# State 0 of the selective scan split into two halves of the tokens, the first half issued in the scan's prologue

## The chip, the core and the metric

The kernel runs on one core of a Trainium2 chip. The time is the device time of one launch in microseconds; smaller is better. The core has five engines that each work through their own queue in order and meet at semaphores: TensorE (PE), VectorE (DVE), ScalarE (ACT), GpSimd (POOL) and SyncE (SP, which only issues DMAs here).

## What is computed

The reference is six residual blocks on x of 4 sequences x 256 tokens x 128 features: a linear attention, a cross attention, a two-pass mixture of experts, a selective state-space scan, a second cross attention and a quantised feed-forward. The change lies in the scan, whose reference is

```python
def _L1_attn_ref(x, W_xproj, W_dt, b_dt, A_log, D):
    proj = x @ W_xproj
    dt_inter = proj[..., :DT_RANK]
    B_ssm = proj[..., DT_RANK:DT_RANK + STATE]
    C_ssm = proj[..., DT_RANK + STATE:]
    delta = jax.nn.softplus(dt_inter @ W_dt + b_dt)
    A = -jnp.exp(A_log)
    log_delta_A = jnp.clip(delta[..., None] * A[None, None], LOG_EPS, CLAMP)
    delta_A = jnp.exp(log_delta_A)
    delta_B_u = delta[..., None] * B_ssm[:, :, None, :] * x[..., None]
    log_dA = jnp.log(jnp.clip(delta_A, 1e-07, None))
    log_R = jnp.cumsum(log_dA, axis=1)
    R = jnp.exp(jnp.minimum(log_R, CLAMP))
    exp_neg_log_R = jnp.exp(jnp.minimum(-log_R, CLAMP))
    S = jnp.cumsum(delta_B_u * exp_neg_log_R, axis=1)
    h = R * S
    y = jnp.einsum('bln,bldn->bld', C_ssm, h) + x * D
    return y
```

STATE is 16: for each of 16 states and each of 128 features a recurrence runs along the 256 tokens of each sequence.

## The kernel before

The 128 features lie on the partitions and the 1024 tokens (4 sequences of 256) along the free dimension. A "half" is 512 tokens, two whole sequences, which is also one bank of PSUM; DELTA, DX, XNT, DA, DXB, CARRY, FLOOR and ROW are all 128 x 1024, and no recurrence crosses from one half to the other. Names of tiles in the profile are those of the memory they lie in: DELTA, DX and LA are parts of SCR, DA and FIRST_STEP of OT, BC, BCOL and DXB of KSA, HH, CCOL and the scratch of the rows of VA, HC of E, and ROW, FLOOR, CARRY and Y are pairs of banks of PS.

**Prologue**, once for each half. It begins when that half's tokens have been normalised by DVE (line 1780), turned by PE (1787) and copied to XNT by ACT (1792). PE projects them to the 64 step inputs (1958), ACT copies these (1979), PE makes four copies of the 32 rows of B and C (1966) and projects the steps to delta (1974). ACT computes the exp and ln of the softplus (1985, 1987, 1988). DVE splits the rows into three bfloat16 parts in BC (2006, 2007, 2011, 2017, 2018, 2019), adds up delta (2025, 2032) and multiplies it by the input into DX (2038). The first half's prologue is done while the experts' last steps still run, apart from lines 2032 and 2038; the second half's stands in front of the scan.

**The loop** goes over the states n = 0 to 15. For each n ACT makes the decays DA = exp(delta * A[n]) (2117) and writes the four entries of FLOOR that start the sequences (2111, out of FIRST_STEP, which lines 2185, 2121 and 2189 prepare for all states at once); POOL clamps DA (2144); DVE carries the reciprocal of the product along with a scan (2201), multiplies it by the input product DXB (2207) and runs the second scan, the state itself (2214). PE spreads one row of B or C over all partitions (356, called by `row`), ACT copies it out of PSUM (2098, 2105), POOL forms the next state's DXB (2151) and the output product (2159), which PE adds up over the states (2061). Only for state 0 does DVE itself form DXB, straight from PSUM (2195).

The order on each engine is the order in which the code is written (`scan_tensor`, `scan_scalar`, `scan_pool`, `scan_vector` and the engines' main lists at the end of the file). On PE, `turn_over` (line 345) issues matmuls whose result nobody reads; 20 of them stand between the end of the experts and the turning of the last half. In DVE's list for state 0 the order is

```python
carry(0); first_input(); accumulate(0); advance(0)
```

and PE's first row of state 1 waits for `dxb`, that is for `first_input`, since it overwrites the banks that this reads.

## Time and profile before

| | us |
|---|---|
| median of 3 runs | 564.98 |
| lowest and highest of them | 563.54, 565.07 |
| profiled execution, its time | 563.37 |
| its span, first to last instruction | 561.6 |
| DVE busy in the span | 448.7 |
| PE busy in the span | 481.0 |
| ACT busy in the span | 277.6 |
| POOL busy in the span | 202.9 |

The profiled execution is the lower end of the runs, 1.61 us under their median; 1.77 us of its time lie around the span. The experts end at about 307.5 us of the span, the scan's loop lies between 325.4 and about 422 us. A busy share says little about such a stretch: several engines hand work to each other there, and the question at each point is which of them was waited for last. All times in the rows further down are microseconds from the span's start.

### The profile page before, as it was taken

The numbers are of one execution on the slowest core, as the hardware profiler recorded it, in microseconds if no ns is written. First come the engines' busy times: TensorE is split into PE (matmuls) and PEld (weight loads), VectorE is DVE, ScalarE is ACT, GpSimd is POOL, SyncE is SP. The second block draws the span as 40 slices with busy tenths as digits, with TensorE's granted clock in tenths as the row PEclk, the third lists the DMA queues.
The fourth block names the chain that finished last, engine by engine and source line by source line (L and its number), as shares of the span: only waits on it lengthen the run. The fifth ranks groups of instructions, "written<-read, shape, count | busy, mean of one in ns | idle before, by whom it ended". The sixth has DMA issues, their size and how long they took to land.

```text
span 561.6 us, 9242 instructions
## 1 busy us (share of the span) xinstructions
PE 481.0 (86%) x3108; PEld 281.3 (50%) x3117; DVE 448.7 (80%) x1176; ACT 277.6 (49%) x517; POOL 202.9 (36%) x170
## 2 busy tenths in 40 slices
PE   7889899999998999899989636656679999999866
PEld 6444666666555666566555102212224656666423
DVE  7998867776587567375886799999996889998996
ACT  3740356555543234345243246555421477777655
POOL 8724000000002305332500048999990255543130
PEclk9999899999999999999999856788789999999989
DMA  5510260000010302422100000000001000000001
GB/s 147 146 39 1 73 191 2 2 1 2 1 48 9 98 11 70 115 61 61 55 0 2 1 0 0 0 0 1 1 0 47 2 2 2 1 3 2 1 1 39
DMA packets 25392, 17.34 MB, mean 31 GB/s; under 512 B 2977, under 2 KB 24162, under 8 KB 25346
## 3 DMA queue, kind: packets, MB, share of 16 engines
q1 hardware_dynamic: 24322, 14.65, 9.2%
q0 software_dynamic: 1024, 2.10, 1.2%
q8 instruction: 26, 0.43, 0.3%
q14 instruction: 20, 0.16, 0.1%
HBM read 10.06 MB, written 5.51 MB: 28 GB/s over the span
## 4 chain that ended last, share of the span: by engine, by line
PE 32%; DVE 16%; POOL 12%; issue 6%; ACT 3%; DMA 1%; SPq 0%; DVEq 0%; POOLq 0%; ACTq 0%
PE PS L1343 7%; PE PS L814 5%; POOL E L2159 4%; PE PS L1385 4%; PE PS L859 3%; POOL KSA L2151 3%; PE PS L876 3%; DVE PS L2201 2%; PE PS L2061 1%; POOL OT L2617 1%; POOL OT L2144 1%; DVE VA L2214 1%; POOL sorted L2607 1%; PE PS L345 1%; PE PS L834 1%
## 5 line engine op out<-in xcount | busy, mean ns | idle before, releaser
L859 PE MATMUL PS<-QM,KP 32*128 32x256 f32 x512 | 91.8, 398 | 1.2 <-ACT E L1047 0.8
L814 PE MATMUL PS<-KP,QP 32*128 32x256 f32 x512 | 78.0, 400 | 0.2 <-ACT QP L1025 0.2
L1047 ACT ACTIVATE E<-PS 128x512 f32<-128x512 f32 x100 | 56.1, 595 | 34.9 <-PE PS L859 24.3
L2607 POOL DMA_INDIRECT sorted<-VA,slot_of x16 | 15.7, 981 | 146.6 <-DVE expert_at L1737 129.6
L859 PEld LDWEIGHTS PS<-QM,KP 32*128 32x128 f32 x512 | 60.5, 184 | 6.2 <-issue 4.8
L356 PE MATMUL PS<-KSA,select 128*128 128x512 bf16 x62 | 25.2, 495 | 40.9 <-ACT KSA L2098 29.1
L1343 PE MATMUL PS<-XNT,KSA 128*128 128x512 f32 x128 | 58.6, 596 | 0.0
L814 PEld LDWEIGHTS PS<-KP,QP 32*128 32x128 f32 x512 | 51.3, 184 | 14.4 <-issue 10.0
L1122 DVE CUSTOM_DVE_ANT_0 SCR<-PS,KSA 128x256 f32<-128x256 f32 x128 | 47.5, 419 | 9.1 <-PE PS L814 8.3
L1117 DVE TENSOR_REDUCE MXT<-PS 128x2 f32<-128x512 f32 x64 | 41.0, 685 | 15.5 <-PE PS L814 15.5
L2582 POOL TENSOR_TENSOR VA<-VA,KSA 128x512 f32<-128x512 f32 x28 | 35.2, 1277 | 37.7 <-ACT VA L1052 37.7
L1351 ACT ACTIVATE E<-PS 128x512 f32<-128x512 f32 x32 | 18.8, 596 | 46.7 <-PE PS L1343 46.7
L2061 PE MATMUL PS<-E,ident 128*128 128x512 f32 x60 | 36.8, 748 | 2.0 <-POOL E L2159 2.0
L2201 DVE TENSOR_TENSOR_SCAN PS<-OT,PS 128x1024 f32<-128x1024 f32 x16 | 36.7, 2295 | 1.4 <-ACT PS L2111 0.8
L356 PEld LDWEIGHTS PS<-KSA,select 128*128 128x128 bf16 x64 | 5.1, 108 | 64.7 <-ACT KSA L2098 39.0
L2151 POOL TENSOR_TENSOR KSA<-SCR,KSA 128x1024 f32<-128x1024 f32 x15 | 35.2, 2348 | 4.8 <-ACT KSA L2098 4.8
L2159 POOL TENSOR_TENSOR E<-VA 128x1024 f32<-128x1024 f32 x15 | 35.3, 2350 | 2.5 <-PE PS L2061 1.5
L1357 DVE TENSOR_TENSOR E<-E,PS 128x512 f32<-128x512 f32 x32 | 21.9, 685 | 17.4 <-ACT E L1351 15.8
L1385 PEld LDWEIGHTS PS<-KSA,E 128*128 128x128 f32 x256 | 30.7, 192 | 10.1 <-issue 9.8
L2144 POOL TENSOR_SCALAR OT<-OT 128x1020 f32<-128x1020 f32 x16 | 16.7, 1042 | 50.7 <-ACT OT L2117 49.6
L2214 DVE TENSOR_TENSOR_SCAN VA<-OT,PS 128x1024 f32<-128x1024 f32 x15 | 34.3, 2286 | 0.5
L345 PE MATMUL PS<-wq,identb 128*128 128x512 bf16 x130 | 34.3, 398 | 0.4 <-issue 0.2
(334 smaller groups left out, 1049.4 us busy)
## 6 DMA issues: line engine op xcount, KB each, us to landing
KSA<-in_w SPq DMA_DIRECT2D x2, 1024.0 KB, 7.0
sorted<-zeros SPq DMA_DIRECT2D x2, 960.0 KB, 6.4
answers<-OT SPq DMA_DIRECT2D x14, 128.0 KB, 1.8
KSA<-in_w SPq DMA_DIRECT2D x2, 512.0 KB, 9.7
QP<-sorted SPq DMA_DIRECT2D x4, 256.0 KB, 3.0
QP<-sorted SPq DMA_DIRECT2D x2, 448.0 KB, 4.7
X<-in_x SPq DMA_DIRECT2D x2, 256.0 KB, 3.3
SCR<-in_ctxT SPq DMA_DIRECT2D x1, 512.0 KB, 6.0
```

Source lines behind the costliest of these rows:

```text
L345: pe.matmul(bank(bk), identb[:, :], wq1[:, :], start=True, stop=True)
L814: ins = pe.matmul(score_bank(n, i)[:, q * S:(q + 1) * S], QP[rows(i), g, t:t + P], KP[rows(i), g, b * S:(b + 1) * S], start=True, stop=Tru ...
L859: ins = pe.matmul(o[:, kt * S:(kt + 1) * S], KP[rows(i), g, t:t + P], QM[rows(i), g, b * S:(b + 1) * S], start=True, stop=True, skip_group ...
L1047: act.activation(slot(m, j), drain_bank(L, m, j), ACT.Exp).then_inc(sig("exps"), 1)
L1117: ins = dve.tensor_reduce(MXT[:, n % 2, :, c], o, AX, ALU.max, negate=True)
L1122: ins = dve.tensor_tensor_reduce(out=BIASED[:, i % 2, q, :], in0=o[:, q, :], in1=BIASQ[:, q, :], scale=-1.0, scalar=3e38, op0=ALU.add, op1 ...
L1343: ins = pe.matmul(unit_bank(g, o), w[:, e, c * P:(c + 1) * P], XNT[:, tokens_of(p)], start=True, stop=True)
L1385: ins = pe.matmul(bank(6)[:, t * P:(t + 1) * P], E6[:, (2 * m + c) % 4, t * P:(t + 1) * P], W2[:, m % NE, c, :], start=(c == 0), stop=(c = ...
L2061: ins = pe.matmul(bank(6 + half), ident[:, :], HC[n % 2][:, half * HALF:(half + 1) * HALF], start=(n == 0), stop=False, skip_group_check=True)
L2151: pool.tensor_tensor(DXB[n % 2], DX, BCOL[n % 2], ALU.mult).then_inc(sig("dxb"), 1)
L2159: pool.tensor_tensor(HC[n % 2], HH[n % 2], CCOL[n % 2], ALU.mult).then_inc(sig("outputs"), 1)
L2201: dve.tensor_tensor_scan(CARRY, DA[n % 3], FLOOR, 0.0, ALU.mult, ALU.add).then_inc(sig("carried"), 1)
```

## The change

State 0's chain is written out by halves. `first_log`, `first_max`, `first_input` and `first_carry` on DVE, `first_step`, `first_decay` and `first_half` on ACT, `first_clamp` on POOL and `scan_first_row` on PE each do one half, 512 tokens or two sequences, of what one instruction did for all 1024. The first half of each is issued in the prologue: on PE right after the experts, on ACT before the second half's softplus, on DVE before the second half's rows are split. The second half stands where the whole stood, but that DVE's carried scan comes behind `scan_rows_tail` together with `first_input`. Three banks of the second half's prologue move to make room (`SCAN_BANK`), and the counts that the later waits ask for go up by one. States 1 to 15 are as before.

```diff
-        SCAN_BANK = ((7, 7, 7), (0, 4, 1))
+        SCAN_BANK = ((7, 7, 7), (1, 6, 7))
...
+        def scan_first_row(pe, half):
+            pe.wait_ge(sig("bc_rows"), half + 1)
+            pe.matmul(bank(half), select[:, 0:1].to_broadcast([P, P]), BC[:, tokens_of(half)], start=True, stop=True)\
+                .then_inc(sig("row_psum"), 1)
+
...
-            pe.wait_ge(sig("bc_rows"), 2)
-
             def row(k, r):
 
                 if k == 1:
-                    pe.wait_ge(sig("dxb"), 1)
-                elif k:
+                    pe.wait_ge(sig("dxb"), 2)
+                else:
                     pe.wait_ge(sig("row_read"), k - 1)
                 project(pe, 0, select[:, r:r + 1].to_broadcast([P, P]), BC, "row_psum")
...
-            row(0, 0)
+            scan_first_row(pe, 1)
             row(1, 1)
...
-            scan_steps_take(act, 1)
-            scan_softplus(act, ch, 1)
...
-                act.wait_ge(sig("row_psum"), n + 1 + max(n - 1, 0))
+                act.wait_ge(sig("row_psum"), n + 2 + max(n - 1, 0))
                 if n >= 2:
-                    act.wait_ge(sig("dxb"), n - 1)
+                    act.wait_ge(sig("dxb"), n)
...
+            def first_step(half):
+                act.wait_ge(sig("first_log"), half + 1)
+                s = FIRST_STEP[:, :, 2 * half:2 * half + 2]
+                act.activation(s, s, ACT.Exp, bias=ssmc[:, 2:3]).then_inc(sig("first_exp"), 1)
+
+            def first_decay(half):
+                act.wait_ge(sig("delta"), half + 1)
+                b = slice(2 * half, 2 * half + 2)
+                act.activation(inner(DA[0])[:, b, :], inner(DELTA)[:, b, :], ACT.Exp, scale=amat[:, 0:1])\
+                    .then_inc(sig("decay"), 1)
+
+            def first_half(half):
+                act.wait_ge(sig("first_max"), half + 1)
+                b = slice(2 * half, 2 * half + 2)
+                act.activation(starts(FLOOR)[:, b, :], FIRST_STEP[:, 0, b].unsqueeze(2), ACT.Copy)\
+                    .then_inc(sig("first"), 1)
+
             def first(n):
 
-                if n:
-                    act.wait_ge(sig("carried"), n)
+                act.wait_ge(sig("carried"), n + 1)
...
-            act.wait_ge(sig("first_log"), 1)
-            act.activation(FIRST_STEP, FIRST_STEP, ACT.Exp, bias=ssmc[:, 2:3]).then_inc(sig("first_exp"), 1)
-            act.wait_ge(sig("delta"), 2)
-            decay(0)
-            act.wait_ge(sig("first_max"), 1)
-            first(0)
+            first_step(0)
+            first_decay(0)
+            first_half(0)
+            scan_steps_take(act, 1)
+            scan_softplus(act, ch, 1)
+            first_step(1)
+            first_decay(1)
+            first_half(1)
             decay(1)
             b_copy(1)
             c_copy(0)
...
+            def first_clamp(half):
+                pool.wait_ge(sig("decay"), half + 1)
+                a = inner(DA[0])[:, 2 * half:2 * half + 2, :]
+                pool.tensor_scalar(a, a, GUARD, LOWEST, ALU.min, ALU.max).then_inc(sig("da"), 1)
+
             def clamp(n):
 
-                pool.wait_ge(sig("decay"), n + 1)
+                pool.wait_ge(sig("decay"), n + 2)
...
-            clamp(0)
+            first_clamp(0)
+            first_clamp(1)
             pool.wait_ge(sig("dx"), 2)
...
+            def first_log(half):
+                b = slice(2 * half, 2 * half + 2)
+                dve.tensor_tensor(FIRST_STEP[:, :, b],
+                                  starts(DELTA)[:, b, :].rearrange("p b o -> p o b").to_broadcast([P, NS, 2]),
+                                  amat[:, :].unsqueeze(2).to_broadcast([P, NS, 2]), ALU.mult).then_inc(sig("first_log"), 1)
+
+            def first_max(half):
+                s = FIRST_STEP[:, :, 2 * half:2 * half + 2]
+                dve.wait_ge(sig("first_exp"), half + 1)
+                dve.tensor_scalar(s, s, LOWEST * GUARD, None, ALU.max).then_inc(sig("first_max"), 1)
+
+            def first_input(half):
+                t = tokens_of(half)
+                dve.wait_ge(sig("row_psum"), half + 1)
+                dve.wait_ge(sig("dx"), half + 1)
+                dve.tensor_tensor(DXB[0][:, t], DX[:, t], bank(half), ALU.mult).then_inc(sig("dxb"), 1)
+
+            def first_carry(half):
+                t = tokens_of(half)
+                dve.wait_ge(sig("da"), half + 1)
+                dve.wait_ge(sig("first"), half + 1)
+                dve.tensor_tensor_scan(CARRY[:, t], DA[0][:, t], FLOOR[:, t], 0.0, ALU.mult, ALU.add)\
+                    .then_inc(sig("carried"), 1)
+
+            scan_delta(dve, 0)
+            first_log(0)
             ch.link(dve.memset(FLOOR, 0.0))
-            scan_delta(dve, 0)
             scan_drive(dve, 0)
+            first_max(0)
+            first_input(0)
+            first_carry(0)
             scan_rows_head(dve, ch, 1)
             scan_positive(dve, ch, 1)
             scan_rows_middle(dve, 1)
             scan_delta(dve, 1)
-            dve.tensor_tensor(FIRST_STEP, starts(DELTA).rearrange("p b o -> p o b").to_broadcast([P, NS, B]),
-                              amat[:, :].unsqueeze(2).to_broadcast([P, NS, B]), ALU.mult).then_inc(sig("first_log"), 1)
+            first_log(1)
             scan_drive(dve, 1)
-            dve.wait_ge(sig("first_exp"), 1)
-            dve.tensor_scalar(FIRST_STEP, FIRST_STEP, LOWEST * GUARD, None, ALU.max).then_inc(sig("first_max"), 1)
+            first_max(1)
             scan_rows_tail(dve, ch, 1)
-
-            def first_input():
-                dve.wait_ge(sig("row_psum"), 1)
-                dve.wait_ge(sig("dx"), 2)
-                dve.tensor_tensor(DXB[0], DX, ROW, ALU.mult).then_inc(sig("dxb"), 1)
+            first_carry(1)
+            first_input(1)
 
...
-                dve.wait_ge(sig("da"), n + 1)
-                dve.wait_ge(sig("first"), n + 1)
+                dve.wait_ge(sig("da"), n + 2)
...
-                dve.wait_ge(sig("carried"), n + 1)
-                dve.wait_ge(sig("dxb"), n + 1)
+                dve.wait_ge(sig("carried"), n + 2)
+                dve.wait_ge(sig("dxb"), n + 2)
...
-                carry(n)
-                if n == 0:
-                    first_input()
+                    carry(n)
                 accumulate(n)
...
@@ -2773,6 +2819,7 @@
             self_tensor(pe)
             cross_tensor(pe, 0)
             experts_tensor(pe)
+            scan_first_row(pe, 0)
             turn_over(pe, 1, 20)
             half_turn(pe, 1, 5)
             turn_over(pe, 1, 2)
```

The queue of DVE between the normalisation of the last half (1780) and the split of its rows (2006, 2007). Names left of the arrow are the output's memory; a scan is printed as SCALAR_TENSOR_TENSOR.

```order
 L1780 TENSOR_SCALAR XN<-X,mv,rstd 128x128 x4
-L2178 MEMSET PS 128x1024
 L2032 TENSOR_TENSOR SCR<-SCR 128x512
+L2205 TENSOR_TENSOR OT<-SCR,amat 128x16x2
+L2229 MEMSET PS 128x1024
 L2038 TENSOR_TENSOR SCR<-SCR,XNT 128x512
+L2212 TENSOR_SCALAR OT<-OT 128x16x2
+L2218 TENSOR_TENSOR KSA<-SCR,PS 128x512
+L2224 SCALAR_TENSOR_TENSOR PS<-OT,PS 128x512
 L2006 CAST KSA<-PS 128x512
 L2007 TENSOR_TENSOR VA<-PS,KSA 128x512
```

Four instructions (the first half of FIRST_STEP's product and maximum, of the input product, and of the carried scan) have come in ahead of line 2006. The memset of FLOOR is the same one, one place later.

The queue of DVE from the second half's middle rows to state 0's accumulation, before and then changed:

```order
L2011 CAST VA<-VA 128x512
L2032 TENSOR_TENSOR SCR<-SCR 128x512
L2185 TENSOR_TENSOR OT<-SCR,amat 128x64
L2038 TENSOR_TENSOR SCR<-SCR,XNT 128x512
L2189 TENSOR_SCALAR OT<-OT 128x64
L2017 COPY KSA<-VA 32x512
L2018 TENSOR_TENSOR VA<-VA 128x512
L2019 COPY KSA<-VA 32x512
L2201 SCALAR_TENSOR_TENSOR PS<-OT,PS 128x1024
L2195 TENSOR_TENSOR KSA<-SCR,PS 128x1024
L2207 SCALAR_TENSOR_TENSOR PS<-PS,KSA 128x1024
```

```order
L2011 CAST VA<-VA 128x512
L2032 TENSOR_TENSOR SCR<-SCR 128x512
L2205 TENSOR_TENSOR OT<-SCR,amat 128x16x2
L2038 TENSOR_TENSOR SCR<-SCR,XNT 128x512
L2212 TENSOR_SCALAR OT<-OT 128x16x2
L2017 COPY KSA<-VA 32x512
L2018 TENSOR_TENSOR VA<-VA 128x512
L2019 COPY KSA<-VA 32x512
L2224 SCALAR_TENSOR_TENSOR PS<-OT,PS 128x512
L2218 TENSOR_TENSOR KSA<-SCR,PS 128x512
L2255 SCALAR_TENSOR_TENSOR PS<-PS,KSA 128x1024
```

The number of instructions is the same; four of them are half as wide.

The queue of ACT from the copy of the last half into XNT to the end of the prologue:

```order
 L1792 ACTIVATE XNT<-PS 128x512
+L2111 ACTIVATE OT<-OT,ssmc 128x16x2
+L2116 ACTIVATE OT<-SCR,amat 128x2x255
+L2122 ACTIVATE PS<-OT 128x2
 L1979 ACTIVATE SCR<-PS 64x512
 L1985 ACTIVATE SCR<-PS,ssmc 128x512
 L1987 ACTIVATE SCR<-SCR 128x512
 L1988 ACTIVATE SCR<-SCR 128x512
-L2121 ACTIVATE OT<-OT,ssmc 128x64
-L2117 ACTIVATE OT<-SCR,amat 128x4x255
-L2111 ACTIVATE PS<-OT 128x4
```

Three instructions have come in ahead of line 1979, and behind 1988 the same three stand again for the other half. On POOL two clamps of 128 x 510 stand in the place of one of 128 x 1020.

## Rows read from the trace of the kernel before

**Rows 1.** The page's first line.

```profile
span 561.6 us, 9242 instructions
```

**Rows 2.** Busy time by stage: stretch, length, busy by engine, granted clock, DMA share, GB/s.

```profile
313.70:318.50 4.80, 4.77 (x17) 1.44 (x18) 2.30 (x3) 1.19 (x2) 0.00 (x0) 0.64 0.00 0
333.40:420.00 86.60, 54.10 (x116) 18.78 (x119) 85.06 (x45) 45.68 (x57) 82.09 (x44) 0.78 0.00 0
```

**Rows 3.** The chain of waits, 313 to 334 us: start, length, piece.

```profile
315.57 1.89 PE PS L1958 x2
...
324.37 0.88 issue
...
328.97 1.05 PE PS L356 x2
...
330.04 1.03 ACT KSA L2098
```

**Rows 4.** Waits of DVE, 325 to 420 us: in total, times, longest.

```profile
DVE PS L2201 <- ACT PS L2111: 0.8, 1, 0.8
```

**Rows 5.** The timeline of DVE, 313 to 330 us.

```profile
313.88 0.91 DVE L2178 MEMSET PS<- 128x1024 f32 x1 [0.21 <-issue]
...
318.52 0.69 DVE L2006 CAST KSA<-PS 128x512 bf16<-128x512 f32 x1 [2.21 <-PE PS L1966]
...
320.27 0.75 DVE L2025 TENSOR_SCALAR SCR<-PS,ssmc 128x512 f32<-128x512 f32 x1 [0.33 <-ACT SCR L1985]
...
322.31 0.26 DVE L2185 TENSOR_TENSOR OT<-SCR,amat 128x64 f32<-128x64 f32 x1
...
323.60 0.69 DVE L2018 TENSOR_TENSOR VA<-VA 128x512 bf16<-128x512 f32 x1
324.33 1.00 DVE L2019 COPY KSA<-VA 32x512 bf16<-32x512 bf16 x1
325.37 2.30 DVE L2201 TENSOR_TENSOR_SCAN PS<-OT,PS 128x1024 f32<-128x1024 f32 x1
327.69 1.22 DVE L2195 TENSOR_TENSOR KSA<-SCR,PS 128x1024 f32<-128x1024 f32 x1
329.02 1.23 DVE L2207 SCALAR_TENSOR_TENSOR PS<-PS,KSA 128x1024 f32<-128x1024 f32 x1
```

**Rows 6.** The timeline of ACT and of POOL, 313 to 325 us.

```profile
314.76 0.60 ACT L1792 ACTIVATE XNT<-PS 128x512 f32<-128x512 f32 x1 [3.10 <-PE PS L1787]
317.56 0.59 ACT L1979 ACTIVATE SCR<-PS 64x512 f32<-64x512 f32 x1 [2.20 <-PE PS L1958]
...
322.86 1.13 ACT L2117 ACTIVATE OT<-SCR,amat 128x1020 f32<-128x1020 f32 x1
...
324.07 2.24 POOL L2144 TENSOR_SCALAR OT<-OT 128x1020 f32<-128x1020 f32 x2 [48.62 <-ACT OT L2117]
```

**Rows 7.** Single lines: duration in ns min/median/max, first and last start, forms.

```profile
L2230 DVE TENSOR_TENSOR_SCAN VA<-OT,PS x2: 1194/1207/1220, 419.9 to 421.0; 128x512 f32<-128x512 f32 x2
...
L2019 DVE COPY KSA<-VA x2: 285/645/1005, 306.7 to 324.3; 32x512 bf16<-32x512 bf16 x2
...
L2144 POOL TENSOR_SCALAR OT<-OT x16: 1037/1037/1122, 324.1 to 411.9; 128x1020 f32<-128x1020 f32 x16
```

**Rows 8.** The timeline at 251 us: POOL and DVE side by side, then DVE's next.

```profile
251.30 0.61 POOL L2758 TENSOR_SCALAR KSA<-SCR 128x512 f32<-128x512 f32 x1
251.33 0.59 DVE L269 TENSOR_TENSOR rt<-rs 128x4 f32<-128x4 f32 x1 [0.18 <-POOL rs L2625]
...
251.95 0.16 DVE L270 TENSOR_TENSOR rt<-rt,ve 128x4 f32<-128x4 f32 x1
```

**Rows 9.** The timeline of PE behind the loop, and the clock there by stretches.

```profile
423.04 1.88 PE L2080 MATMUL PS<-E,ident 128*128 128x512 f32 x4
...
416.30:419.70 3.40, 3.18 (x6) 1.09 (x6) 3.37 (x2) 0.20 (x1) 3.40 (x2) 0.50 0.00 0
419.70:426.00 6.30, 6.10 (x22) 2.77 (x21) 4.98 (x7) 0.00 (x0) 1.57 (x2) 1.00 0.00 0
```

More of the change, by code:

```diff
@@ L2089, in scan_scalar @@
         def scan_scalar(act, ch):
-            scan_steps_take(act, 1)
-            scan_softplus(act, ch, 1)
             def b_copy(n):
-                act.wait_ge(sig("row_psum"), n + 1 + max(n - 1, 0))
+                act.wait_ge(sig("row_psum"), n + 2 + max(n - 1, 0))
                 if n >= 2:
-                    act.wait_ge(sig("dxb"), n - 1)
+                    act.wait_ge(sig("dxb"), n)
                 act.activation(BCOL[n % 2], ROW, ACT.Copy).then_inc(sig("row_read"), 1)
             def c_copy(n):
-                act.wait_ge(sig("row_psum"), b_rows(n + 1) + n + 1)
+                act.wait_ge(sig("row_psum"), b_rows(n + 1) + n + 2)
                 if n >= 2:
@@ L2184, in scan_vector @@
             scan_delta(dve, 1)
-            dve.tensor_tensor(FIRST_STEP, starts(DELTA).rearrange("p b o -> p o b").to_broadcast([P, NS, B]),
-                              amat[:, :].unsqueeze(2).to_broadcast([P, NS, B]), ALU.mult).then_inc(sig("first_log"), 1)
+            first_log(1)
             scan_drive(dve, 1)
-            dve.wait_ge(sig("first_exp"), 1)
-            dve.tensor_scalar(FIRST_STEP, FIRST_STEP, LOWEST * GUARD, None, ALU.max).then_inc(sig("first_max"), 1)
+            first_max(1)
             scan_rows_tail(dve, ch, 1)
-            def first_input():
-                dve.wait_ge(sig("row_psum"), 1)
-                dve.wait_ge(sig("dx"), 2)
-                dve.tensor_tensor(DXB[0], DX, ROW, ALU.mult).then_inc(sig("dxb"), 1)
+            first_carry(1)
+            first_input(1)
             def carry(n):
-                dve.wait_ge(sig("da"), n + 1)
-                dve.wait_ge(sig("first"), n + 1)
+                dve.wait_ge(sig("da"), n + 2)
+                dve.wait_ge(sig("first"), n + 2)
                 dve.tensor_tensor_scan(CARRY, DA[n % 3], FLOOR, 0.0, ALU.mult, ALU.add).then_inc(sig("carried"), 1)
             def accumulate(n):
-                dve.wait_ge(sig("carried"), n + 1)
-                dve.wait_ge(sig("dxb"), n + 1)
+                dve.wait_ge(sig("carried"), n + 2)
+                dve.wait_ge(sig("dxb"), n + 2)
                 dve.scalar_tensor_tensor(CARRY, CARRY, 1.0, DXB[n % 2], ALU.min, ALU.mult).then_inc(sig("input"), 1)
```

## The prediction

> **What bounds the kernel now.** I read the page's span first (561.6 us, [rows 1]), then the stages around the change, then the chain of waits through them, then each engine's timeline where the chain changes hands. In the scan's loop, 333.4 to 420 us, DVE is busy for 85.06 of 86.60 us and POOL for 82.09, PE for 54.10 [rows 2]: DVE sets the pace and POOL is close behind. DVE waits once in it, 0.8 us for ACT's line 2111 ahead of state 1's first scan [rows 4]. So the loop is a rigid block: whoever starts it earlier ends it earlier, and what follows hangs on its end.
>
> In front of the loop DVE is not the pace-maker all the time. Behind line 2038 of the first half it sits idle for 2.21 us until PE's four copies of the rows arrive at 318.52 [rows 5]. In that gap PE runs L1958 for 1.89 us [rows 3], at a granted clock that averages 0.64 over 313.70 to 318.50 [rows 2]. Before line 2025 DVE idles another 0.33 us, for ACT [rows 5]. From 322 us on DVE is on the chain without a pause: the copy of line 2019 (1.00 us), state 0's first scan (2.30), the input product of line 2195 (1.22), and 2207 starts at 329.02 [rows 5]. The end of 2195 also releases PE's first row of state 1 (328.97, 1.05 us), ACT's copy (330.04, 1.03 us), one more row and copy, and so state 1 [rows 3]. What ends 2195 earlier therefore moves the whole rest.
>
> **The copy of line 2019.** It has a price of its own kind. The same 32 x 512 copy took 285 ns in the first half and 1005 ns in the second [rows 7]; the second time POOL's clamp ran from 324.07 [rows 6], for 1.122 us, the longest of 16 [rows 7], so to 325.19, and the copy ended at 325.33, 0.14 behind it. The chain calls 0.88 us of it "issue" [rows 3]: DVE stood still with its instruction issued. The other order is in the rows too: line 2018 (0.69 us, from 323.60) had begun before the clamp, and it was the clamp that took 1.122 instead of 1.037 us [rows 5, 7]. Whoever begins first goes on; the second stands.
>
> **The change, part by part.**
>
> *First half on DVE, ahead of line 2006.* Added work: half of line 2185 (0.26 for 64 columns, so 0.2), half of 2189 (0.2), an input product of 128 x 512 (0.69, as line 2018, the nearest two-operand row of that width [rows 5]), and a scan of 128 x 512, 1.19 us by line 2230 [rows 7]. Sum 2.3 us, plus some 0.03 us between instructions: about 2.4. The cover is the 2.21 us gap and the 0.33 us behind it [rows 5]. Step by step, with DVE starting where it did (313.88): delta to 314.6, product 314.8, memset (0.91) to 315.75, drive to 316.5. Meanwhile ACT is free at 315.36, behind line 1792 [rows 6]; its exp of the starts takes 0.3 and the half decay 0.6 (a 128 x 512 ACT row is 0.60, a 128 x 1020 one 1.13 [rows 6]), so DA's first half stands at 316.3 and POOL clamps it to 316.95 at 0.61 us, the price of a 128 x 512 tensor_scalar [rows 8]. DVE: maximum 316.55 to 316.7, input product to 317.4, scan to 318.65; line 2006 then begins at 318.65 instead of 318.52. These 0.13 us go into the 0.33 us of idle in front of line 2025 [rows 5]. ACT's three added pieces end at 316.9, before PE has the steps for line 1979 at 317.56 [rows 6]. **Net zero on the path.** The cover has a hole: if POOL's clamp begins before DVE's maximum, the maximum stands until some 316.85 and line 2006 slips to 319.0; 0.2 of the 0.5 us would show. PE's added matmul stands in front of 20 that nobody reads and a wait, so at nothing. It might even help there: if that bit of work kept the clock from averaging 0.64 over the stretch [rows 2], L1958 would take half a microsecond or more less and line 2006 could come up to 0.3 us earlier, as soon as DVE is through with its added work. Bounds: nothing, or 0.3 us gained; I take nothing, since the work is small.
>
> *The copy of line 2019.* ACT's decay of the second half now starts at 322.8 and ends 0.5 us sooner (0.6 in the place of 1.13 us [rows 6]), at 323.4; POOL begins its half clamp at 323.5, 0.07 before line 2018 would begin (323.57: the narrower product of line 2185 saves 0.03). I take it that line 2018 gets through first, since POOL's clamp was slowed by 0.085 us while 0.22 us of it lay beside line 2018 [rows 5, 7], so that it seems to need the memory only 0.1 us or so after its start. Then 2018 ends at 324.26, the clamp at 324.7, and the copy at 324.83 to 324.88: **0.45 us earlier** than 325.33. Were there no clash at all it would end at 324.6 (0.73 earlier); the other bound is the first rival.
>
> *Half a scan.* In place of 2.30 us [rows 5] a scan of 1.19 [rows 7]: **1.1 us less**.
>
> *Half an input product.* In place of 1.22 a product of 0.69 [rows 5]: **0.53 us less**. PE's row for it needs BC at 324.9 and one matmul of about 0.5 us (two took 1.05 [rows 3]), ready at 325.5, while DVE's half scan lasts until 326.1.
>
> Sum: 0.45 + 1.1 + 0.53 = 2.1 us, so line 2207 begins at 326.9. The chain of rows and copies to state 1 hangs on the input product and moves by the same 2.1; so do DVE's 0.8 us of waiting there and everything of POOL's. POOL's first full clamp then lies at 324.7 to 325.8, beside a scan; line 2201 took its 2.30 us beside the second clamp, and half a scan was 1.19 [rows 5, 7], so it was not slowed. No queue is refilled and no DMA is moved: SP's list is the same. **What is late next** is the same handover to state 1.
>
> Against its own time the profiled execution would come to 563.37 - 2.1 = 561.3 us. It lies 1.6 under the median of the three runs; against that median the forecast is 564.98 - 2.1 = **562.9 us**, 0.37% less.
>
> **A rule to weigh.** The trace shows a DVE instruction with two operands in SBUF, the tiny line 269, taking 0.59 us beside a POOL tensor_scalar that had begun 0.03 us earlier, where its neighbour of the same shape took 0.16 [rows 8]. The Trainium skill, "SBUF — State Buffer", section "Who interferes with whom", says that a VectorE instruction with both inputs in SBUF contends with a GpSimd instruction that reads SBUF, and that the one that begins second is fully blocked. Line 2018 is such an instruction. By the row of the old kernel, where it came first, the sum is 2.1; by the rule with POOL's half clamp first, it is that of the first rival.
>
> **The rivals.**
>
> *1. Line 2018 and the copy both lose to POOL.* The half clamp now becomes ready 0.07 us before line 2018, where the whole one came 0.47 us after its start (324.07 against 323.60 [rows 5, 6]). If POOL wins, line 2018 stands until about 324.0 and ends at 324.7; by then ACT has the decay of state 1 ready (1.13 us from 323.5), POOL's full clamp can begin at 324.73, and if it beats the copy by a hair, that ends 0.14 us behind it, at 325.9. The scan starts 1.0 us later than forecast, the gain is 1.1: 563.9 us. For it: three starts within 0.1 us. Against: it takes two lost races in a row; with the first alone the gain is 2.0.
>
> *2. The first half is not covered.* If the half clamp costs the full clamp's 1.04 us [rows 7] and the maximum stands behind it, DVE's scan ends at 319.4, line 2006 starts 0.9 us late and some 0.7 shows: gain 1.4, 563.6 us. Against: the 0.61 us of [rows 8] for half the columns.
>
> *3. The loop does not follow.* State 1 would be held by something that has not moved, and the change gives nothing: 565.0 us. I find no such thing; everything that state 1 waits for comes behind the input product [rows 3].
>
> *4. Slower: the clock behind the loop.* PE's matmuls that end the sums stand on the path: L2080's four took 1.88 us, and L2061's four before them the same, at a granted clock of 1.00, which rose from 0.50 at 419.7 [rows 9]. The changed kernel brings them 2.1 us nearer to where the clock was low. If it rises only behind them, they cost twice: 3.8 us more, against 2.1 gained, so 1.7 slower, 566.7 us; it decides from 2.1 us on, when more than half of them run at 0.50. For it: only 1.6 us lie between the rise and the first of them. Against: the matmuls that nobody reads in front of them are what kept PE busy for 3.18 of the 3.40 us before the clock rose [rows 9], and they move along.
>
> **How the numbers follow.** Forecast 0.62 (561.0 to 563.6 with the runs' own spread of 1.5 us), rival 1 0.15, rival 2 0.12, rival 3 0.05, rival 4 0.06. The range must reach over rivals 1 and 2, and below to the profiled execution's 561.3 and the 0.3 us that PE's clock might add: 561.0 to 564.7. About 0.3%, 1.7 us, is what a measurement of this kernel tells from no change. The forecast lies only 0.4 us beyond it. Faster: nearly all of the forecast (0.58) and a little of rival 2: 0.60. Same: the rest of the forecast, rivals 1 to 3: 0.34. Slower: rival 4, 0.06.
>
> **What would show it.** In the changed trace: line 2006 within 0.2 us of 4.64 us behind the first DVE instruction after the normalisation (318.52 against 313.88 [rows 5]) and no DVE idle of 2.2 us before it; the scan of line 2224's second half starting about 324.9 and the accumulation at 326.9, on this time axis; the second copy of line 2019 at 0.5 us or so instead of 1.00; the loop's length unchanged. Wrong would be: the copy at 1 us again or line 2018 above 0.69 (rival 1); line 2006 late by more than 0.3 (rival 2); a wait of DVE inside the loop that was not there (rival 3); the eight fp32 matmuls behind the loop above 1.88 us a group (rival 4).

## The result and the profile after

The changed kernel takes 560.11 us (median of 10 runs, 558.89 to 561.56), the kernel before, on the same chip, 563.92 (10 runs, 561.85 to 565.07): ratio 0.993, 95% interval 0.9913 to 0.9946. That is faster, by 3.8 us where 2.1 were forecast. Both kernels were run again three times: the medians were 563.6 to 563.9 us for the old one and 559.8 to 560.1 for the new one. A few executions of the runs below took 632 us or more; they are in no median and no ratio.

One view of each engine carries the comparison. First the timeline of DVE in the changed kernel; it answers to [rows 5] (columns as there):

```profile
311.46 1.12 DVE L1780 TENSOR_SCALAR XN<-X,mv,rstd 128x128 f32<-128x128 f32 x4
...
313.62 0.91 DVE L2229 MEMSET PS<- 128x1024 f32 x1 [0.21 <-issue]
...
315.17 0.59 DVE L2212 TENSOR_SCALAR OT<-OT 128x32 f32<-128x32 f32 x1
315.67 0.68 DVE L2218 TENSOR_TENSOR KSA<-SCR,PS 128x512 f32<-128x512 f32 x1
316.27 1.22 DVE L2224 TENSOR_TENSOR_SCAN PS<-OT,PS 128x512 f32<-128x512 f32 x1
317.40 0.67 DVE L2006 CAST KSA<-PS 128x512 bf16<-128x512 f32 x1
...
318.71 0.74 DVE L2025 TENSOR_SCALAR SCR<-PS,ssmc 128x512 f32<-128x512 f32 x1
...
319.83 0.69 DVE L2032 TENSOR_TENSOR SCR<-SCR 128x512 f32<-128x512 f32 x1
...
321.77 0.69 DVE L2018 TENSOR_TENSOR VA<-VA 128x512 bf16<-128x512 f32 x1
322.49 0.58 DVE L2019 COPY KSA<-VA 32x512 bf16<-32x512 bf16 x1
323.10 1.23 DVE L2224 TENSOR_TENSOR_SCAN PS<-OT,PS 128x512 f32<-128x512 f32 x1
324.36 0.69 DVE L2218 TENSOR_TENSOR KSA<-SCR,PS 128x512 f32<-128x512 f32 x1
325.16 1.23 DVE L2255 SCALAR_TENSOR_TENSOR PS<-PS,KSA 128x1024 f32<-128x1024 f32 x1
...
329.55 2.30 DVE L2249 TENSOR_TENSOR_SCAN PS<-OT,PS 128x1024 f32<-128x1024 f32 x1 [0.83 <-ACT PS L2128]
```

The 2.21 us of idle in front of line 2006 are gone, and so is the 0.33 in front of 2025: DVE works from the normalisation to state 0's end almost without a pause (0.21 us at the memset). Line 2006 still stands 4.82 us behind the end of line 1780 (312.58), as before (318.52 - 313.68 = 4.84). The copy of line 2019 takes 0.58 us instead of 1.00. State 1's first scan begins 16.97 us behind the end of line 1780; in the old trace it was 19.74 (333.42 less 313.68). I call this **the stretch**; its 2.8 us are the change's own part. POOL's two half clamps and the first whole one, which answer to [rows 6]:

```profile
314.82 0.91 POOL L2162 TENSOR_SCALAR OT<-OT 128x510 f32<-128x510 f32 x1 [40.46 <-ACT OT L2116]
321.79 1.14 POOL L2162 TENSOR_SCALAR OT<-OT 128x510 f32<-128x510 f32 x1 [6.07 <-ACT OT L2116]
323.01 1.04 POOL L2168 TENSOR_SCALAR OT<-OT 128x1020 f32<-128x1020 f32 x1
```

Both half clamps began beside a DVE instruction with two operands in SBUF and took 0.3 and 0.5 us longer than the 0.61 that such a clamp took alone (its row stands with the run that has the zeros on ScalarE, below). DVE's maximum (line 2212, 0.59 us instead of 0.18) stood behind the first of them.

The timeline of PE ahead of and in the second half's prologue shows what the forecast had not counted:

```profile
306.44 4.48 PE L345 MATMUL PS<-wq,identb 128*128 128x512 bf16 x20
312.63 0.66 PE L1787 MATMUL PS<-ident,XN 128*128 128x128 f32 x4 [1.72 <-DVE XN L1780]
313.12 0.60 PE L345 MATMUL PS<-wq,identb 128*128 128x512 bf16 x2
314.07 1.04 PE L1958 MATMUL PS<-XNT,wssm 128*64 128x512 f32 x2 [0.35 <-ACT XNT L1792]
```

L1958's pair takes 1.04 us where it had taken 1.89 in the chain [rows 3]. The granted clock, by stretches as in [rows 2], is 1.00 here and was 0.64 there. By a **fall** of the clock I mean in what follows a time in which it is at 0.50, the lower of its two levels (1.2 of 2.4 GHz). The loop in the second row is unchanged (DVE 84.93 of 86.50 us):

```profile
312.58:317.40 4.82, 3.99 (x18) 1.23 (x18) 4.54 (x7) 2.10 (x5) 0.91 (x1) 1.00 0.01 2
...
329.50:416.00 86.50, 52.27 (x115) 18.51 (x119) 84.93 (x45) 45.59 (x57) 81.74 (x44) 0.80 0.00 0
```

DVE's waits from 311 to 416 us are the same one at state 1 as in [rows 4], and the memset's:

```profile
DVE PS L2249 <- ACT PS L2128: 0.8, 1, 0.8
DVE PS L2229 <- issue: 0.2, 1, 0.2
```

The matmuls behind the loop run as in [rows 9]: L2083, which was L2080, takes 1.88 us again.

```profile
419.41 1.88 PE L2083 MATMUL PS<-E,ident 128*128 128x512 f32 x4
```

The spans differ by 3.4 us (558.2 and 561.6). The stretch gives 2.8. Another 1.1 us were gained ahead of line 1780, where the code is the same, and 0.4 lost behind the loop.

### The profile page after: what moved, and what is told of

Read it like the earlier page. It is cut to its first block, busy times and chain, and to the rows that moved or that the text cites. A ratio compares the mean times of both kernels' runs of the same rounds, so it can differ in the third digit from the quotient of the medians.

```text
span 558.2 us, 9251 instructions
## 1 busy us (share of the span) xinstructions
PE 475.9 (85%) x3108; PEld 279.4 (50%) x3117; DVE 448.2 (80%) x1180; ACT 277.9 (50%) x520; POOL 203.8 (37%) x171
## 4 chain that ended last, share of the span: by engine, by line
PE 31%; DVE 21%; POOL 8%; issue 6%; ACT 3%; DMA 1%; SPq 0%; DVEq 0%; POOLq 0%; ACTq 0%
PE PS L1343 7%; PE PS L814 5%; PE PS L1385 4%; DVE PS L2249 3%; PE PS L859 3%; DVE VA L2262 3%; POOL E L2183 3%; PE PS L876 3%; POOL KSA L2175 2%; PE PS L2064 2%; DVE PS L2255 2%; POOL OT L2663 1%; POOL sorted L2653 1%; PE PS L834 1%; DMA answers<-OT 1%
## 5 line engine op out<-in xcount | busy, mean ns | idle before, releaser
L859 PE MATMUL PS<-QM,KP 32*128 32x256 f32 x512 | 91.9, 398 | 1.2 <-ACT E L1047 0.8
L859 PEld LDWEIGHTS PS<-QM,KP 32*128 32x128 f32 x512 | 60.6, 184 | 6.2 <-issue 4.8
L1122 DVE CUSTOM_DVE_ANT_0 SCR<-PS,KSA 128x256 f32<-128x256 f32 x128 | 47.5, 420 | 9.1 <-PE PS L814 8.3
L356 PE MATMUL PS<-KSA,select 128*128 128x512 bf16 x60 | 23.6, 481 | 35.4 <-ACT KSA L2099 30.7
L1351 ACT ACTIVATE E<-PS 128x512 f32<-128x512 f32 x32 | 18.8, 596 | 46.7 <-PE PS L1343 46.7
L2249 DVE TENSOR_TENSOR_SCAN PS<-OT,PS 128x1024 f32<-128x1024 f32 x15 | 34.4, 2295 | 1.3 <-ACT PS L2128 0.8
L876 PE MATMUL PS<-E,VX 128*32 128x256 f32 x512 | 34.3, 385 | 0.1
L1343 PEld LDWEIGHTS PS<-XNT,KSA 128*128 128x128 f32 x128 | 22.8, 191 | 22.7 <-issue 22.4
```

The lines of the kernel that those rows point to most:

```text
L859: ins = pe.matmul(o[:, kt * S:(kt + 1) * S], KP[rows(i), g, t:t + P], QM[rows(i), g, b * S:(b + 1) * S], start=True, stop=True, skip_group ...
L876: ins = pe.matmul(bank(6)[rows(i), (g % 2) * S:(g % 2) * S + S], VX[:, QT * b + kt, HG * g + i, :], slot(m, j)[:, kt * S:(kt + 1) * S], st ...
L1122: ins = dve.tensor_tensor_reduce(out=BIASED[:, i % 2, q, :], in0=o[:, q, :], in1=BIASQ[:, q, :], scale=-1.0, scalar=3e38, op0=ALU.add, op1 ...
L1343: ins = pe.matmul(unit_bank(g, o), w[:, e, c * P:(c + 1) * P], XNT[:, tokens_of(p)], start=True, stop=True)
L2249: dve.tensor_tensor_scan(CARRY, DA[n % 3], FLOOR, 0.0, ALU.mult, ALU.add).then_inc(sig("carried"), 1)
```

## The experiments

Three accounts were open: **moved work** (the forecast's 2.1 us, the rest chance), **the clock ahead of the last half** (worth something more because it stayed up), and something in **code that is the same**. A table of all runs comes at the end of this section.

### Both kernels again

> The kernel before, unchanged, timed against itself for the size of the noise. Three accounts of the 3.8 us are open. Moved work: 2.1 us come from half a scan, half a product and the shorter copy, and anything else is chance. Clock ahead of the last half: TensorE's clock fell to 0.50 at 313.9 us in the old trace and did not in the new one, worth 0.7 us where it falls. Early stretch: 1.5 us were gained at 41 to 47 us, where the code is the same. Chance would have this run's trace differ from the old one in those two places about as often as not, and the ratio 1.000 within 0.002. If the old kernel always falls there, this trace shows 0.50 at 40.8 to 44.2 and at 313.9 to 317.3 again.

> The changed kernel, unchanged. Moved work alone: about 2.1 us under the kernel before (0.996), in any trace from the end of line 1780 to state 1's first scan about 17.5 us where the clock has fallen and 17.0 where not. With a clock effect that is systematic: 3 to 4.5 us (0.992 to 0.995), 17.0 us in that stretch, and no fall of the clock at about 313.

No edit. The old kernel against itself: 1.0006 (0.9988 to 1.0025), the changed one 0.9921 (0.9891 to 0.9951). In the stretch the old kernel's clock had fallen again (19.8 us), the new one's had not (17.0); the fall at about 41 us, ahead of anything that the change touches, is in the first and fourth trace of the old kernel and in the second and third of the changed one, and in none of their other four. So what the early part of the kernel takes is chance: the end of line 1780 lay between 311.2 and 314.8 us in the four traces of the changed kernel, between 311.7 and 313.7 in the four of the old one. The fall at 41 us is one of three in that part, the others lie at about 11 and 57 us. In the one trace of the eight without any of them line 1780 ended at 311.2 us, in the four with one at 311.7 to 312.6, in the two with two at 313.7 and in the one with all three at 314.8.

### Filling TensorE's idle ahead of the last half

```diff
-            turn_over(pe, 1, 20)
+            turn_over(pe, 1, 28)
```

> The kernel before with 28 instead of 20 matmuls that nobody reads ahead of the turning of the last half, 8 x 0.21 us into TensorE's 1.9 us of idle. Clock ahead of the last half: the clock stays at 1.00, L1958's pair takes 1.0 instead of 1.9 us, the rows arrive 1.2 us earlier, and the kernel gains 0.7 to 1.2 us (about 0.998). Moved work only: 0, ratio 1.000; slower by up to 0.3 us if the last of them are in the way.

0.9969 (0.9945 to 0.9994) and a stretch of 18.5 us: no fall, line 2006 at 3.6 instead of 4.8 us behind the end of line 1780. The clock account holds: in the old kernel the fall costs 1.3 us of the stretch. (As a time the ratio says 1.7 us, with an interval from 0.3 to 3.1.) The same in the changed kernel, 27 for 20:

> The changed kernel with 27 instead of 20 such matmuls. If in the changed kernel the clock never falls there, the same time as the changed kernel within 0.3 us. If it falls in some executions, up to 0.5 us less. If the matmuls stand in the way of the turning, up to 0.3 us more.

0.9925 (0.9898 to 0.9952), stretch 17.0: nothing left to gain, as the clock was up already.

### How little it takes

> The kernel before with 21 instead of 20 matmuls that nobody reads ahead of the last half's turning: one matmul of 0.21 us more on TensorE, which is what the change puts there too with its row of state 0. If the change's extra gain comes from that one matmul: no fall of the clock ahead of the last half, the stretch from the end of line 1780 to state 1's first scan takes 18.5 us instead of 19.8, and the kernel gains 1.3 us (0.998), as with 28. If the change keeps the clock up by something else, the clock falls as before: 19.8 us and 1.000.

1.0001 (0.9981 to 1.0021), and the trace had the fall (stretch 20.1 us). By this the one matmul was nothing. It was tried again, and with 23:

> The kernel before with 21 instead of 20 matmuls that nobody reads, once more. Up to the turning of the last half TensorE then does exactly what it does in the changed kernel, whose clock stayed up there in 4 of 4 traces, as the old one's fell in 4 of 4. If the length of the idle (1.72 instead of 1.93 us) decides, this trace has no fall, 18.5 us for the stretch, and the ratio lies below 1 by some tenths of a per cent. If it falls again and the ratio is 1.000 again, the one matmul is not what keeps the clock up in the changed kernel.

> The kernel before with 23 such matmuls, 0.64 us more than before and 0.43 more than with 21. Between 21 (ratio 1.000) and 28 (0.997). If the idle's length decides, it is at 0.997 already and its trace has no fall (18.5 us); otherwise it lies between.

The second trace with 21 had no fall (18.5 us) and its ratio was 0.998 (0.9955 to 1.0005). With 23 it was **0.9941** (0.9919 to 0.9964), no fall. By that ratio three matmuls that nobody reads bring the old kernel 3.3 us, more than was expected and nearly what the change brings. But these are six executions with an interval from 2.0 to 4.6 us; the stretch of 18.5 us, the same as with 28, shows 1.3 of it, and the kernel with 28 gained 1.7. PE in the kernel with 23:

```profile
306.13 5.13 PE L345 MATMUL PS<-wq,identb 128*128 128x512 bf16 x23
312.54 0.66 PE L1787 MATMUL PS<-ident,XN 128*128 128x128 f32 x4 [1.28 <-DVE XN L1780]
...
313.97 1.04 PE L1958 MATMUL PS<-XNT,wssm 128*64 128x512 f32 x2 [0.35 <-ACT XNT L1792]
```

The idle of PE ahead of L1787 was 1.93 us in the old kernel, 1.72 with 21 and in the changed kernel, 1.28 with 23. Over all twenty traces: with 1.93 us the clock fell there in 4 of 6 (the four unchanged old kernels; not in the two with delays below, which are the same up to there), with 1.72 in 1 of 10, with less in 0 of 3; the kernel with 12 matmuls, below, had 3.44 us and the fall. By these counts one matmul more seems to make the fall rarer; it does not abolish it. The two traces without the fall at 1.93 us were taken on one chip and the old kernel's three repeated ones on two others, so chance and chip are not told apart here.

### The changed kernel with the clock down

```diff
-            turn_over(pe, 1, 20)
+            turn_over(pe, 1, 12)
```

> The changed kernel with 12 instead of 20 such matmuls: TensorE idles 1.7 us more ahead of the last half, so that the clock should fall there. If the moved work is worth 2.1 us at the old clock, as forecast, the stretch takes 17.7 us (19.8 less 2.1) against 17.0 now, and the kernel loses 0.7 us against the changed one: about 0.994 to 0.996 of the kernel before. If the stretch stays at 17.0, the clock has no part in it. If it takes 18.2 or more, the clock explains half of the whole gain.

0.9952 (0.9932 to 0.9972); stretch 17.57 us. This is the clean test of the forecast, since the clock is down here too (from about 312 us, with L1787 at 1.12 us and L1958's pair at 1.75). DVE's timeline:

```profile
311.31 1.12 DVE L1780 TENSOR_SCALAR XN<-X,mv,rstd 128x128 f32<-128x128 f32 x4
...
317.20 0.69 DVE L2006 CAST KSA<-PS 128x512 bf16<-128x512 f32 x1 [0.16 <-PE PS L1966]
...
318.94 0.75 DVE L2025 TENSOR_SCALAR SCR<-PS,ssmc 128x512 f32<-128x512 f32 x1 [0.33 <-ACT SCR L1985]
...
320.27 0.69 DVE L2032 TENSOR_TENSOR SCR<-SCR 128x512 f32<-128x512 f32 x1
```

The added work fits under the gap with 0.16 us to spare, the 0.33 us in front of line 2025 are back, and the stretch is 19.74 - 17.57 = **2.17 us** shorter than the old one, for a forecast of 2.1.

### The first half not moved

```diff
             first_max(0)
-            first_input(0)
-            first_carry(0)
             scan_rows_head(dve, ch, 1)
...
             scan_rows_tail(dve, ch, 1)
+            first_carry(0)
+            first_input(0)
             first_carry(1)
             first_input(1)
```

> The changed kernel with state 0's input product and carried scan of the first half put back behind the second half's rows: the same halves on the same engines, but nothing of DVE's big work moved into the prologue. Moved work: the line 2006 comes at once behind PE, 3.6 us behind the end of line 1780 instead of 4.8, state 0's accumulation comes later by 1.9 us less the 0.6 us that the second half's delta now comes sooner, so 1.3 us more in the stretch (18.3 us) and 1.3 us slower than the changed kernel. If the moved work were worth nothing and the clock all, the same time as the changed kernel.

0.996 (0.9939 to 0.9981), median 561.3 us; stretch 18.6. The halves alone bring the stretch nothing beside an old kernel with its clock up (18.5); moving them brings 1.6 us of it.

### FLOOR's zeros from ScalarE

```diff
-            ch.link(dve.memset(FLOOR, 0.0))
             scan_drive(dve, 0)
...
             norm_root(act, ch, 3, tiles_of(1))
+            ch.link(act.activation(PS[:, 2:4, :].rearrange("p a (b n) -> p (a b) n", b=4),
+                                   zeros[:, :].unsqueeze(1).to_broadcast([P, 8, P]), ACT.Copy))
```

> The changed kernel with FLOOR filled with zeros by ScalarE in its idle time ahead of the last half, instead of VectorE's memset of 0.91 us between the first half's product and drive. If the first half's added work does not fit under the gap once the clock stays up (line 1780 to the second half's delta is 7.25 us, and 6.66 in the filled kernel before), this gives back up to 0.6 us: the maximum no longer stands behind POOL's clamp (0.18 instead of 0.59 us), line 2006 comes at 4.1 instead of 4.8 us, delta at 6.7, the stretch takes 16.4 us. If the added work was covered, no change.

Each step came as expected: line 2006 at 4.1 us, delta at 6.7, the maximum no longer behind POOL, the stretch 16.45 us, 0.5 less. In its timeline the maximum and what follows it read

```profile
316.86 0.18 DVE L2212 TENSOR_SCALAR OT<-OT 128x32 f32<-128x32 f32 x1 [0.23 <-ACT OT L2111]
316.96 0.68 DVE L2218 TENSOR_TENSOR KSA<-SCR,PS 128x512 f32<-128x512 f32 x1
318.16 1.23 DVE L2224 TENSOR_TENSOR_SCAN PS<-OT,PS 128x512 f32<-128x512 f32 x1 [0.53 <-POOL OT L2162]
```

and the first half clamp, which here began beside no DVE instruction with two operands in SBUF,

```profile
317.52 0.61 POOL L2162 TENSOR_SCALAR OT<-OT 128x510 f32<-128x510 f32 x1 [40.53 <-ACT OT L2116]
```

The time did not follow: 0.9932 (0.9902 to 0.9961), the changed kernel's own. Half a microsecond is too small for these runs; in this trace 0.7 us were lost right behind the loop (see under the count). No version beat the changed kernel.

### Delays, for what lies behind the loop

The old kernel's three later traces had a second fall, in the end of the last cross attention, where the code is the same. PE's timeline in the fourth trace of the old kernel:

```profile
514.87 1.93 PE L876 MATMUL PS<-E,VX 128*32 128x256 f32 x16
516.73 1.11 PE L886 MATMUL PS<-ident,OT 128*128 128x128 f32 x4
```

And the clock there, by the view of stretches with the columns of [rows 2]:

```profile
514.20:517.60 3.40, 3.40 (x27) 1.55 (x24) 1.57 (x3) 2.69 (x5) 0.00 (x0) 0.57 0.01 2
```

In the changed kernel's first trace the same two lines take 1.07 and 0.66 us:

```profile
512.92 1.07 PE L876 MATMUL PS<-E,VX 128*32 128x256 f32 x16
513.93 0.66 PE L886 MATMUL PS<-ident,OT 128*128 128x128 f32 x4
```

PE was busy without a gap before this fall (9.20 of the 9.20 us from 505.00 to 514.20). What follows L834's last pair then takes 47.9 us instead of 46.4: 1.5 us. To see whether the moment at which a kernel gets there matters, both kernels were delayed in the loop:

```diff
+                if n in (2,):
+                    for j in range(NT):
+                        dve.bn_stats(st[:, j, :], X[:, j, :])
                 accumulate(n)
```

and once more with `(2, 5)`. Each delay turned out as 1.40 us of loop (from state 1's first scan to the end of the last one 88.76, 90.16, 91.55 us).

> The kernel before with 8 needless bn_stats on VectorE in the loop's state 2, a pure delay of 1.6 us on the engine that sets the pace. The traces so far show a second fall of TensorE's clock, at 512 to 517 us, in the end of the last cross attention, worth 1.3 us: in 2 of 3 traces of kernels that reach the loop like the old one, in none of the 3 like the changed one. Account with this fall (whether it comes depends on when the kernel gets there): a delay of 1.6 us moves the old kernel away from it, so the kernel loses only 0.5 to 1.0 us, and its trace has no fall there. Account without: it loses 1.6 us.

> The same delay twice (states 2 and 5), 3.2 us. With the fall: its effect comes and goes with the delay, so that here the old kernel meets it about as often as undelayed, and loses 3.2 us, that is 2.2 to 2.7 us more than with one delay. Without: 3.2 us as well, 1.6 more than with one.

> The changed kernel with the delay of 1.6 us. With the fall: this puts the changed kernel where the old one was, so the fall at about 515 us appears in its trace and it loses 1.6 plus up to 1.3, 2.3 to 2.9 us against the changed kernel (0.9975 to 0.999 of the kernel before). Without: it loses 1.6 us (0.996).

> The changed kernel with 3.2 us of delay. With the fall: it is gone again, the kernel loses 3.2 us against the changed one, only 0.3 to 0.9 more than with one delay. Without: 3.2 us, 1.6 more than with one.

The old kernel with 1.4 us of useless work was not slower: 0.9988 (0.997 to 1.0006). With 2.8 us it was at 1.0034 (1.001 to 1.0058), 1.9 us slower with an interval from 0.6 to 3.3. The changed kernel went from 0.993 to 0.9961 (0.9938 to 0.9984) and 0.9982 (0.9962 to 1.0002): 1.7 and 2.9 us for 1.4 and 2.8. So the account's half on the old kernel agrees with the times, and its half on the changed one does not agree with the traces: one delay did not bring the fall to the one that was taken (46.6 us behind L834), two did (48.0 us), against the expectation. One trace says little, though: of the eleven executions with one delay seven took 559.0 to 561.7 us and four 563.4 to 564.9, and the trace is of the first group. Neither delayed old kernel's trace had a fall, here or ahead of the last half. The place ahead of the last half was not in the delay's power, since it lies before it, so part of what the delays seem to have cost the old kernel too little is chance there.

### The count

> The kernel before once more, for its trace: which of the two falls of the clock it has. The falls account says that the old kernel meets one at 312 to 315 us or one at 512 to 517 us in most executions: the stretch from the end of line 1780 to state 1's first scan takes 19.8 (fall) or 18.5 us (none), and what follows L834's last turning of the maxima takes 47.9 (fall) or 46.5 us.

> As the run before it. If neither fall shows in these two traces and the medians stay at 563.8, the falls don't explain the 3.7 us, and 1.5 us of it are without a cause.

> The changed kernel once more, for its trace: 17.0 us for the stretch and 46.5 us for the end, both without a fall, 3.7 us under the kernel before. A fall at about 515 us here would say that the changed kernel meets it too, and its part of the gain would shrink.

> The changed kernel a fourth time, with the same two numbers expected: 17.0 us for the stretch and 46.5 us for the end, no fall in either.

Ratios 0.9995 twice (0.998 to 1.0011 and 0.998 to 1.001), then 0.9914 (0.9896 to 0.9932) and 0.9933 (0.9912 to 0.9954). Both old traces had both falls, the one ahead of the last half and the one behind L834. Of the new ones, the fourth had neither; the third had the fall behind the loop, longer than the old kernel's: there L859's 16 matmuls take 2.11 us as well.

```profile
513.90 1.93 PE L876 MATMUL PS<-E,VX 128*32 128x256 f32 x16
515.77 1.12 PE L886 MATMUL PS<-ident,OT 128*128 128x128 f32 x4
516.82 2.11 PE L859 MATMUL PS<-QM,KP 32*128 32x256 f32 x16
```

There is a third place in code that is the same, right behind the loop. From the start of the last two scans (L2230, in the changed kernel L2276) to L834's last pair it is 94.8 us in fifteen of the twenty traces. It is 95.2 in the old kernel's first trace, 95.5 and 95.3 in the changed one's first and fourth, and 95.5 in those of the kernels with 27 matmuls and with the zeros on ACT. In these five, and in no other, the clock was low until within 0.5 us of the start of these scans.

All traces, the stretch and what follows L834's last pair (from the start of its second matmul to the end of the span):

| kernel, traces in order | stretch, us | behind L834, us | median of its runs, us |
|---|---|---|---|
| before: 1, again, third, fourth | 19.7, 19.8, 19.8, 19.9 | 46.4, 47.9, 47.9, 47.9 | 563.9, 563.6, 563.9, 563.8 |
| changed: 1, again, third, fourth | 17.0, 17.0, 17.0, 17.0 | 46.5, 46.4, 49.4, 46.4 | 560.1, 559.9, 560.1, 559.8 |
| before with 21, again | 20.1, 18.5 | 47.9, 46.6 | 564.3, 562.1 |
| before with 23 / 28 | 18.5 / 18.5 | 46.6 / 46.6 | 560.6 / 562.2 |
| before, one delay / two | 18.5 / 18.5 | 46.4 / 46.8 | 563.4 / 565.8 |
| changed with 12 / 27 | 17.6 / 17.0 | 46.6 / 46.5 | 561.0 / 560.5 |
| changed, first half late / zeros on ACT | 18.6 / 16.5 | 48.0 / 46.7 | 561.3 / 560.6 |
| changed, one delay / two | 17.0 / 17.0 | 46.6 / 48.0 | 561.0 / 563.2 |

## Why the prediction was wrong

The direction was right and the cause it named is there, but the forecast of 2.1 us is not: 3.8 were measured, and 560.1 lies under the low end of 561.0. The 2.8 us between 562.9 and 560.1 have two parts. 1.1 of them are the base: the forecast was taken from 564.98, the median of three runs, where ten runs of the same kernel have 563.92. The other 1.7 are the gain.

- *Half a scan, half a product* (1.1 and 0.53 us): right. From the end of the copy of line 2019 to the accumulation there are 2.09 us instead of 3.69, so 1.60.
- *The copy of line 2019* (0.45 us): right, and for the reason given. Line 2018 began at 321.77, the half clamp at 321.79, and it was the clamp that stood; the copy then stood behind it for 0.3 us. From the start of line 2032 to the copy's end it is 3.24 us instead of 3.74: 0.50. The Trainium skill's rule of "SBUF — State Buffer", "Who interferes with whom", that the one that begins second is blocked, agrees with all three places of this kernel: line 2018 kept its 0.69 us, the clamp took 1.14 instead of 0.61, the copy 0.58 instead of 0.28. The clamp was lengthened by 0.53 us where 0.67 of it lay beside line 2018, so by nearly all of the overlap. Rival 1 did not come, in any trace.
- *First half on DVE: net zero on the path*: right with the clock down (2006 at 4.77 us with 12 matmuls against 4.84, and 2.17 us gained over the whole stretch). The hole in the cover, the maximum behind POOL's clamp, was real: 0.41 us. It was not there in the trace with 12 matmuls (the maximum took 0.18 us, just ahead of the clamp); with it the 0.16 us to spare would have become some 0.25 us of delay, by my estimate, so the 2.17 are the upper end of what the moved work brings with the clock down. With the clock up the gap that covers is shorter, since PE is ready 1.2 us sooner, and then 0.6 us of the added work do show: line 2032 at 7.25 us instead of 6.66. So the moved work is worth 2.2 us with the clock down and 1.5 with it up (18.49 - 16.97).
- **The step that failed** is the sentence on PE's added matmul: "Bounds: nothing, or 0.3 us gained; I take nothing, since the work is small." The clock stayed up in all four traces of the changed kernel and fell in all four of the old one, and that matmul is all that PE has more ahead of this place; the two traces with 21 matmuls, one with the fall and one without, leave it likely rather than shown that it alone decides. In the stretch a clock that stayed up was worth 17.57 - 16.97 = 0.6 us on top of the 2.2, together the 2.8 that all four pairs of traces show. The bound of 0.3 was wrong as well: I had let line 2006's start stand for the whole effect, but line 2006 came no earlier at all; what came earlier was the exp and ln of ACT behind L1974, and DVE without its 0.33 us wait in front of line 2025. So one of the prediction's own signs failed: on the old trace's time axis, which is 1.10 us later, the second half's scan began at 324.2 instead of 324.9 and the accumulation at 326.3 instead of 326.9. (Another, 4.64 us from DVE's first instruction behind the normalisation to line 2006, came out at 4.91 only because that first instruction is no longer the memset with its 0.21 us of idle.) With 0.6 in the place of 0.3 the low end would have been 560.7, still above 560.1.
- *The loop follows* and *the clock behind the loop*: the loop is 88.76 us in both, and L2083 took 1.88 us again, as L2080 had. Rivals 3 and 4 did not come. But the clock did matter behind the loop: right there by up to 0.7 us, in either kernel, which is less than rival 4 had feared, and, in favour of the change, 95 us further on than it had looked: in the four traces of each kernel what follows L834 takes 47.5 us in the mean before and 47.2 after, and without the third trace 46.4.

Of the 3.8 us, 2.2 are moved work and a shorter stall, shown by the changed kernel with its clock down; 0.6 are the clock ahead of the last half, shown by the same comparison. That leaves 1.0. By the fall at 512 to 517 us a part of it is explained (0.3 us by the count of four, up to 1.1 if the third trace of the changed kernel was a rare one), and the place right behind the loop takes 0.2 of that back (95.1 us in the mean of the four traces after, 94.9 before). Scatter of the medians is not the rest: the four pairs differ by 3.8, 3.7, 3.9 and 4.1 us. The traces can't show it either, since the executions that were traced differ by less than the others: 561.3 and 558.9 us of span in the mean, 2.4 us.

What all executions do show is their mean granted clock. It is 0.951 over the 29 of the changed kernel and 0.944 over the 36 in which the old one was run again. Within the changed kernel the 12 executions at 0.954 or more took 559.1 us in the mean and the 9 at 0.948 or less 561.3. So a lower clock goes with more time, and the old kernel's is the lower; but a mean doesn't say where it fell, and falls within the loop cost nothing that these runs show. How the 1.0 splits stays open, as does why a delay that should have moved the changed kernel into the fall did not.

## What to carry to other kernels

Work that is split and its half put under a wait pays what the trace's own durations say, if the shared resources are looked at in pairs: who begins first beside whom. Where an engine's clock depends on what it did, an edit's smallest piece on that engine can outweigh the rest, so price both levels of the clock at the place, and try the filler matmuls by themselves: three of them gave the old kernel 2.0 to 4.6 us, where the stretch that they were meant for gained 1.3. Take the base of a forecast from more than three runs, if they differ by as much as the gain. And a gain of a per cent or less deserves several traces, for the same kernel's stretches differ by more than a microsecond between executions.

## What was not expected of the hardware

- TensorE's clock fell to the lower of its two levels (1.2 of 2.4 GHz) after an idle of 1.93 us in 4 of 6 traces, after 1.72 us in 1 of 10; in the end of the cross attention it fell while PE was busy without a gap (9.20 of 9.20 us), on matmuls that use 32 rows or 32 columns of the array (L859, L876).
- 1.4 us of useless work on the engine that sets the pace cost the old kernel nothing measurable (0.9988, 0.997 to 1.0006), 2.8 us cost it 1.9 us (0.6 to 3.3).
- A POOL tensor_scalar of 128 x 510 takes 0.61 us alone (the kernel with the zeros on ACT had it so once), and 0.91 and 1.14 beside a DVE instruction with two SBUF operands that had begun before it.
- The memset of PSUM on DVE (0.91 us) had 0.21 us of idle in front of it in both kernels, in either of its two places.
